# First product of a two-layer convolution kernel: twelve float32r matmuls in a row, then the four float32 ones

## The reference, cut to what matters

```python
k = jnp.einsum('ijk,imk->ijmk', hx, hy)[0]        # separable filter of each channel
y = jnp.fft.irfft2(u_f * k_f, s=(fft_size, fft_size))[..., :L, :L]
out = y + x * bias[:, None, None]                  # layer 0
...
scores = jnp.einsum('bpsd,bptd->bpst', x, x) * inv_dim
red = jnp.sum(scores * weights[None], axis=-1, keepdims=True)
y = x + red
mean = jnp.mean(y, axis=(0, 2, 3), keepdims=True)
var = jnp.var(y, axis=(0, 2, 3), keepdims=True)
y_hat = (y - mean) * jax.lax.rsqrt(var + BN_EPS)   # layer 1
```

## Time and profile before

| | |
|---|---|
| Runs of the kernel | 950.36 us median of 3 (950.07 to 951.35) |
| Profiled execution, its own time | 953.63 us |
| Its span in the profile | 950.9 us |
| Granted TensorE clock, mean of the span | 0.993 |
| PE busy | 930.9 us, 98% |
| PEld busy | 815.0 us, 86% |
| DVE, ACT, POOL busy | 749.4, 682.0, 672.5 us |

### The profile page before, as it was taken

How to read it: one execution, slowest core, us unless ns; L and a number is a source line. 1 busy time by engine, 2 the same in 40 slices (tenths; PEclk the granted TensorE clock), 3 DMA queues, 4 the chain that set the end, 5 groups by cost and what they waited for, 6 DMA issues and landing times.

```text
span 950.9 us, 18901 instructions
## 1 busy us (share of the span) xinstructions
PE 930.9 (98%) x5312; PEld 815.0 (86%) x5312; DVE 749.4 (79%) x2457; ACT 682.0 (72%) x1088; POOL 672.5 (71%) x520
## 2 busy tenths in 40 slices
PE   7999999999999999999999999999999999999994
PEld 5888888888888888888888888888888888888883
DVE  2677887887877888887887887887887878887886
ACT  2447777777677777777777778777777778777776
POOL 2676777776687777777777776776776776776752
PEclk9999999999999999999999999999999999999997
DMA  7767999997899999989798999979799999988954
GB/s 222 265 170 219 251 257 301 261 241 291 228 276 288 208 303 289 272 237 290 199 307 293 213 287 303 267 248 287 228 271 302 246 252 296 274 247 293 256 141 187
DMA packets 91439, 244.09 MB, mean 257 GB/s; under 512 B 17184, under 2 KB 42016, under 8 KB 83232
## 3 DMA queue, kind: packets, MB, share of 16 engines
q1 hardware_dynamic: 73568, 235.73, 85.0%
q10 hardware_dynamic: 17856, 8.20, 3.4%
HBM read 176.52 MB, written 67.37 MB: 256 GB/s over the span
## 4 chain that ended last, share of the span: by engine, by line
PE 78%; POOL 9%; issue 8%; DVE 2%; DMA 1%; ACT 1%; POOLq 0%; DVEq 0%
PE ps_c L525 30%; PE ps_u L525 26%; PE ps_z L525 22%; POOL zl L417 3%; POOL xl L397 3%; POOL toep L390 2%; POOL wl L405 1%; POOL rstd L378 1%; DVE z_sb L718 1%; DMA toep_whole<-filters_padded 1%; DVE ul L758 0%; ACT uh L464 0%; POOL stat L371 0%; DMA par<-params_in 0%; DVE products L731 0%
## 5 line engine op out<-in xcount | busy, mean ns | idle before, releaser
L417 POOL TENSOR_TENSOR zl<-z_sb,zh 128x1024 fp32r<-128x1024 f32 x127 | 304.1, 2395 | 241.1 <-ACT zh L510 241.1
L731 DVE CUSTOM_DVE_ANT_0 products<-z_sb,ps_c 128x256 bf16<-128x256 f32 x504 | 182.2, 418 | 147.7 <-PE ps_c L525 147.7
L485 ACT ACTIVATE out_sb<-z_sb,shift,gain 128x256 f32<-128x256 f32 x496 | 257.3, 591 | 21.1 <-DMA out<-out_sb 15.7
L525 PE MATMUL ps_z<-uh,toep 128*128 128x512 f32 x768 | 271.4, 408 | 0.2 <-DVE z_sb L718 0.2
L464 ACT ACTIVATE uh<-ps_u 128x1024 fp32r<-128x1024 f32 x127 | 130.5, 1028 | 165.9 <-PE ps_u L525 165.9
L525 PE MATMUL ps_u<-toep,xh 128*128 128x256 f32 x1016 | 235.1, 313 | 2.8 <-POOL toep L390 2.4
L525 PE MATMUL ps_c<-zh,wh 128*128 128x512 f32 x504 | 196.3, 390 | 1.3 <-POOL zl L417 1.2
L525 PE MATMUL ps_c<-zh,wl 128*128 128x512 f32 x504 | 196.1, 389 | 0.0
L525 PE MATMUL ps_c<-zl,wh 128*128 128x512 f32 x504 | 196.1, 389 | 0.0
L525 PE MATMUL ps_u<-toep_whole,xt_sb 128*128 128x128 f32 x1016 | 195.8, 274 | 0.0
L742 DVE BATCH_NORM_STATS2 stat<-z_sb 128x6 f32<-128x256 f32 x512 | 179.4, 413 | 0.1
(11 more groups left out here) (79 smaller groups left out, 913.7 us busy)
## 6 DMA issues: line engine op xcount, KB each, us to landing
xt_sb<-xt_in SPq DMA_DIRECT2D x64, 1024.0 KB, 10.8
x_sb<-x_in SPq DMA_DIRECT2D x128, 512.0 KB, 9.1
out<-out_sb SPq DMA_DIRECT2D x124, 512.0 KB, 7.5
w_sb<-wt_in SPq DMA_DIRECT2D x64, 256.0 KB, 7.8
toep_whole<-filters_padded SPq DMA_DIRECT2D x64, 256.0 KB, 7.8
everyone<-partition_moments ACTq DMA_DIRECT2D x62, 128.0 KB, 8.7
out<-z_sb SPq DMA_DIRECT2D x2, 512.0 KB, 3.1
out<-z_sb SPq DMA_DIRECT2D x4, 256.0 KB, 3.4
```

Of the source, the lines that this page charges most:

```text
L417: nc.gpsimd.tensor_tensor(low, z_sb[:, r, h], high.bitcast(F32), ALU.subtract)\
L485: last = nc.scalar.activation(to[:, k, b], z_sb[:, r, h, k, b], ACT.Identity, bias=shift[:, r, g:g + 1], scale=gain[:, r])
L525: return nc.tensor.matmul(o, a, b, start=start, stop=stop)
L731: last = nc.vector.tensor_tensor_reduce(products[:, cs.slot(2), k, b], z_sb[:, r, h, k, b], bank[:, k, b], 1.0 / math.sqrt(SIDE), 0.0, ALU ...
```

## The change

The loop over the four places is split in two. First the twelve float32r matmuls of 256 columns run, three for each place in the same order as before; then the four float32 matmuls of 128 columns, one for each place. With that, the two images of a block h, which share a PSUM bank, are in accumulation at the same time. So the flags now go by bank: start stands only on the very first matmul of a bank (b = 0) and stop on the last of the bank (b = PAIR - 1). No matmul is added or taken away and no operand changes. `u_done` stays on the last matmul of the product.

```diff
-                    for h in range(BLOCKS):
-                        rows = slice(P * h, P * (h + 1))
-                        for b in range(PAIR):
-                            o = u_bank(us)[:, h, b, :]
-                            mm(o, xh[:, s, b, rows], toep[:, t, 1, 0, :], True, False)
-                            mm(o, xh[:, s, b, rows], toep[:, t, 1, 1, :], False, False)
-                            mm(o, xl[:, s, b, rows], toep[:, t, 1, 0, :], False, False)
-                            last = mm(o[:, P:SIDE], xt_sb[:, r, PAIR * us.half() + b, 1, rows],
-                                      toep_whole[:, r, 1, 0:P], False, True)
+                    places = [(h, b, slice(P * h, P * (h + 1))) for h in range(BLOCKS) for b in range(PAIR)]
+
+                    for h, b, rows in places:
+                        o = u_bank(us)[:, h, b, :]
+                        mm(o, xh[:, s, b, rows], toep[:, t, 1, 0, :], b == 0, False)
+                        mm(o, xh[:, s, b, rows], toep[:, t, 1, 1, :], False, False)
+                        mm(o, xl[:, s, b, rows], toep[:, t, 1, 0, :], False, False)
+                    for h, b, rows in places:
+                        last = mm(u_bank(us)[:, h, b, P:SIDE], xt_sb[:, r, PAIR * us.half() + b, 1, rows],
+                                  toep_whole[:, r, 1, 0:P], False, b == PAIR - 1)
                     last.then_inc(u_done, 1)
```

## The result

| | before | changed |
|---|---|---|
| Median of the runs | 951.21 us (7 runs) | 953.51 us (7 runs) |
| Ratio to before, 95% interval | | 1.0024 [1.0014, 1.0034] |
| Span of the profiled execution | 950.9 us | 951.6 us |
| One pair in the loop | 7.113 us | 7.133 us |
| PE busy | 930.9 us | 933.3 us |

The forecast was 948.3 us with 951.8 as the upper end, so the time lies outside the range and on the other side of no change. The page of the changed kernel says that the general picture is the same as in the earlier trace rows: PE full, clock at its upper level.

A forecast was written before the change was run, and what follows sets the result against it. PE's matmul issue was taken to bound the kernel, 7.11 us a pair. First-product terms summed to 2.3015 us against 2.318, 16.5 ns less a pair, times 128 2.1 us: 948.3 us, range 944.5 to 951.8.

The forecast's parts named there:

- What bounds the kernel: Whole loop: PE never waits for another engine, so a pair takes PE's matmul issue time, 7.11 us.
- How a record is read: PE trace: neighbouring records overlap; the 365 ns xh record behind float32 is stamped early, its 82 ns no removable stall.
- duration less 162: PE trace: a matmul's record lasts 162 ns longer than the time to the next start, so subtracting gives spacings.
- ten more spacings: First product, between 256-column matmuls in the row: 117.7 ns each, the xh to xl spacing, 1.177 us in all.
- slower rival: Row of twelve: overlapping weight loads settle the ten spacings at 122 ns, loss above 119.4; 953.8 us, chance 0.1.
- a round trip costs 4 + 4 to 7 ns: First product: price of switching into float32 and back; the change removes three of four round trips a pair.
- The float32 halves: End of the first product: eight halves in a row at 0.111 us each, 0.888 us, bounds 108 and 113 ns.
- the first `xh`: Head of the first product, following the third product as before: 0.115 us.
- the last `xl`: First product, last 256-column matmul before float32: 0.1215 us, as before.
- The faster rival: Row of twelve: spacings settle at 113.4 ns, 59 ns a pair, 7.5 us more gain; 942.9 us, chance 0.2.
- The flags at nothing: First product: the start flag that goes from b = 1 adds and removes no instruction and costs nothing.
- It doesn't do what it says: Rival on PE's instruction order: twelve and four in a row would not appear; no chance given.

The follow-up runs named there:

- e9: Kernel before with the float32 matmul moved to second at each place (xh, float32, xh, xl), flags as before: ratio 0.9973, pair 7.100 us.
- e4: Changed kernel with the second xh and the xl matmul of each place at 128 columns instead of 256: 945.1 us in one execution, pair 7.047 us.
- e1: Kernel before, its order kept, with only the changed kernel's start and stop flags: ratio 1.0004, pair 7.113 us.
- e8: Changed kernel with its four float32 matmuls left out: 899.6 us in one execution; an undisturbed pair 6.22 us.
- e2: Changed kernel with the four float32 matmuls moved between the four first xh and the other eight 256-column matmuls: ratio 0.9986, again 0.9978; pair 7.107 us.
- e3: Half the change to the kernel before: six 256-column matmuls, then two float32, for each block in turn: ratio 1.001, pair 7.127 us.
- e7: Changed kernel with each float32 matmul at 64 columns instead of 128: 953.6 us in one execution, pair 7.133 us.
- e5: Changed kernel with the third product's last eight matmuls alternating with the next pair's first eight 256-column ones: ratio 1.0552, pair 7.55 us.

## Why the prediction was wrong, by its own steps

- **What bounds the kernel: right.** PE bounds, PE waits for nobody in the loop but once for `zl`, and 20 ns in a pair came out as 20 ns times the pairs.
- **How a record is read: right.** The 365 ns record behind float32 is a stamp, not a stall: the changed kernel has none of them on `xh`, and nothing was gained by that. But *duration less 162* is good only to 1 or 2 ns: it gives 121 and 113 where the starts give 120 and 112.
- **The term that failed: "ten more spacings", at 117.7 ns.** They are 119.9 on average, 22 ns more in a pair; with that alone the 16.5 ns of gain become a loss of some 6. The error was to take one link of a chain, `xh` to `xl`, for the pace of a row. In place two it follows a 122 and stands before a 0.13: from the true start, 402.66, to the float32 at 403.03 the three take 0.37 us, read to 0.01; in place one, 402.09 to 402.44, 0.35 us. The prediction's own mean of whole places said it: 0.580 us less two halves of 0.111 leaves 0.358 for three matmuls, 119.3 each, and that is the 119.4 at which its own slower rival starts to lose.
- **Hence "a round trip costs 4 + 4 to 7 ns" is false.** The 121 to 122 ns at the switches are no more than a 256-column matmul takes in a row without any switch (120), and the 117.7 between them was the exception. The twelve of a pair took about 1.43 us before (2.318 less the 0.888 of the float32 halves) and 1.433 in the changed kernel. No saving from three round trips less shows anywhere; e9, which keeps all four, is the fastest of the kernels that do the whole work.
- **The float32 halves: sized 1 ns low.** "8 x 0.111" is 0.895 us, 7 ns more. The difference that mattered was within the spread of the rows: lone halves take 108 to 113, 111 at the median, and the back-to-back ones of the sine network 0.11 to 0.115. Against before, the 10 ns of the first product are, by averaged starts: 5 in the first halves of the four float32 matmuls (113, 108, 108 and 113 ns before, 112 on average after), 4 in the spacings behind the second `xh` and the `xl` of each place, and 1 in the rest. How a lone second half and the `xh` behind it share their 231 ns can't be read, because of the early stamp; so the 110 ns of a lone half, on average, is an estimate.
- **The second and third product: a term I left out.** I took their cost as fixed. They lose 10 ns, because the slow start of the second product lasts longer behind the changed first product, down into the third. The three together, 22 + 7 + 10, less 2 for the first `xh` (113 instead of 115) and the last `xl`, make the 36.5 ns between the 16.5 forecast as gain and the 20 lost.
- **The slower rival had the mechanism** as far as the runs show it (weight loads overlap one another and give a row its pace) and the point at which it decides, 119.4 ns; the row settled at 119.9, just past it. It didn't creep up to 122: it is flat from the third matmul on. So of the 20 ns lost the row alone explains a few, and the float32 halves and the slow start of the second product, which no rival had, explain the rest. I gave this rival 0.1, arguing that the third spacing "is high for its own reason". The faster rival was the least right: nothing approached 113.4 in the row, and the 109 ns that I took from the Trainium skill ("TensorE: Matmul & The Clock Gate", Back-to-back issue gap) even less. That section calls its 262 cycles for 256 columns the gap of an isolated matmul, and says that in a stream of loads and matmuls both set the spacing; the prediction read only the table. Under the same title the Trainium skill gives a weight load as its columns divided by 1.2 GHz, 107 ns for 128 (section LDWEIGHTS); e4 shows 113 from load to load. These two statements, and not the table, were the ones to weigh.
- **The flags at nothing: right** (e1). "It doesn't do what it says": it did.

## What to carry to other kernels

Before pricing a reordering on PE, ask for each matmul whether its columns or the next one's weights take longer. Here loads of 128 stationary columns came 113 ns apart, so going below 256 moving columns brought little (86 ns of a pair in e4, where streaming alone gave 480); whether fewer loads would bring more, no run shows. Take the pace of a row from the mean over a run of links, never from one link. And charge an edit also for what stands behind it: the order inside one product moved the next product by as much as its own.

## What was not expected of the hardware

- 512-column matmuls need five to ten of their kind to reach an even 226.7 ns behind a dense row of short ones (233, 236, 228, 232, 231 in e8). It takes five without float32 directly ahead (e2, e8, e9), seven behind one lone float32 matmul (before), ten behind two or four of them that follow a row at 120 ns (e3, e7, changed), but six behind four that follow the narrowed row of e4. What in PE does this stays open; no run here tells it.
- The spacings are the same to a nanosecond in nearly every pair: 7.133 us in two profiles of the changed kernel, 7.113 in those of before and of e1.
- A 64-column float32 matmul takes as long as one of 128 columns, 112 ns a half (e7).
- A 256-column matmul between 512-column ones is cheaper by some 3 ns, but its neighbour dearer by 5 to 7: 116 to 118 and 232 to 234 in place of 120 and 227 (e5).
